# A decoder's first cross attention pipelined two tiles ahead, its bidirectional attention reordered on f16 rows, and filler products in four gaps of TensorE

## The reference, cut to what matters

```python
x = x + gated_linear_attention(ln(x))                    # 4 heads, chunks of 64 tokens here
x = x + cross_attention(ln(x), ctx)                      # 16 heads of 8, softmax over 77 rows
x = x + moe_block(ln(x))                                 # attention over 2 entries, 8 experts
x = x + attention_with_bias(ln(x))                       # 16 heads of 64, softmax over 512
# bidirectional attention; e = ln(x), q = ctx
Sim = (e@w1)[:, :, None] + (q@w2)[:, None, :] + einsum('bid,bjd->bij', e*w3, q) + b_sim
A = softmax(Sim, axis=2);  hq = A @ q
Batt = softmax(max(Sim, axis=2), axis=1);  hc = Batt @ e
x = x + concat([e, hq, e*hq, e*hc]) @ W_qv + b_qv
# feed-forward with fake quantisation
xs = round(e * 32767/amax(e)) / (32767/amax(e))          # 16-bit activations, 8-bit weights
x = x + quantised(gelu(xs @ W_in_q + b_in)) @ W_out_q + b_out
```

## Time and profile before

| | us |
|---|---|
| median of 3 runs | 480.96 |
| the profiled execution, whole | 480.13 |
| its span (what the rows below are in) | 478.3 |
| PE busy in the span | 437.0 (91%) |
| DVE busy | 365.9 (76%) |
| ACT busy | 285.5 (60%) |
| POOL busy | 211.4 (44%) |

### The profile page before, as it was taken

How to read it: one execution, slowest core, us unless ns; L and a number is a source line. 1 busy time by engine, 2 the same in 40 slices (tenths; PEclk the granted TensorE clock), 3 DMA queues, 4 the chain that set the end, 5 groups by cost and what they waited for, 6 DMA issues and landing times.

```text
span 478.3 us, 13019 instructions
## 1 busy us (share of the span) xinstructions
PE 437.0 (91%) x4502; PEld 307.3 (64%) x4502; DVE 365.9 (76%) x987; ACT 285.5 (60%) x669; POOL 211.4 (44%) x545
## 2 busy tenths in 40 slices
PE   7899878887679999699999999999999998999897
PEld 5354446666566777366667676767666665887656
DVE  3867759997868998887778787777778767566766
ACT  3743525565349876577777777777777767413460
POOL 5150011470023458026766767567766767342200
PEclk9979979999979999999999999999999999999999
DMA  7499925500000231000000000000000000000001
GB/s 216 77 98 99 100 32 176 167 14 2 1 0 14 62 93 35 2 1 18 3 19 1 2 16 16 0 0 0 0 0 0 2 1 1 3 3 0 1 1 45
DMA packets 15622, 15.81 MB, mean 33 GB/s; under 512 B 1348, under 2 KB 12859, under 8 KB 15579
## 3 DMA queue, kind: packets, MB, share of 16 engines
q1 hardware_dynamic: 15579, 15.24, 15.7%
HBM read 10.52 MB, written 4.72 MB: 32 GB/s over the span
## 4 chain that ended last, share of the span: by engine, by line
PE 72%; DVE 20%; ACT 4%; issue 3%; DMA 1%; POOL 0%; SPq 0%; DVEq 0%; POOLq 0%
PE bank L951 16%; PE bank L1461 12%; PE bank L1413 10%; PE bank L1336 5%; PE bank L1244 4%; PE bank L1257 3%; PE bank L1454 3%; PE bank L1332 3%; PE bank L1351 2%; DVE PX L1763 2%; DVE mx L1761 2%; PE bank L1573 1%; PE bank L1053 1%; PE bank L1067 1%; DVE Y L1611 1%
## 5 line engine op out<-in xcount | busy, mean ns | idle before, releaser
L855 ACT ACTIVATE SN<-SN,nmx 128x512 f32<-128x512 f32 x128 | 92.7, 724 | 9.8 <-DVE nmx L1975 7.5
L951 PE MATMUL bank<-cs,SN 128*128 128x128 f32 x512 | 67.3, 274 | 3.3 <-DVE Z L1968 1.6
L951 PEld LDWEIGHTS bank<-cs,SN 128*128 128x128 f32 x512 | 57.2, 141 | 18.1 <-issue 12.1
L1413 PE MATMUL bank<-TK,TQ 64*128 64x512 f16 x384 | 52.6, 379 | 1.6 <-DVE TK L1938 1.6
L549 POOL TENSOR_TENSOR CTW<-YT 128x128 f32<-128x128 f32 x64 | 29.6, 462 | 51.6 <-DVE YT L1973 51.1
L1960 DVE CUSTOM_DVE_ANT_0 SN<-bank,strip 128x512 f32<-128x512 f32 x64 | 43.3, 677 | 1.2 <-PE bank L1413 0.6
L1975 DVE CUSTOM_DVE_ANT_0 SN<-bank,strip 128x512 f32<-128x512 f32 x64 | 43.6, 681 | 0.0
L1968 DVE COPY PTO<-bank 128x512 f32<-128x512 f32 x32 | 22.1, 692 | 20.8 <-PE bank L1461 19.2
L866 ACT COPY PTO<-bank 128x512 f32<-128x512 f32 x32 | 18.8, 586 | 26.1 <-PE bank L1461 26.1
L1968 DVE COPY Z<-bank 128x512 f32<-128x512 f32 x32 | 22.1, 691 | 15.9 <-PE bank L1461 14.1
L1461 PE MATMUL bank<-Z,TV 128*64 128x128 f32 x512 | 33.4, 273 | 0.0
(11 more groups left out here) (317 smaller groups left out, 983.9 us busy)
## 6 DMA issues: line engine op xcount, KB each, us to landing
bias_rows<-biasr SPq DMA_DIRECT2D x1, 4096.0 KB, 45.2
band<-bias_rows SPq DMA_DIRECT2D x1, 3072.0 KB, 12.3
wqkv<-in_twqkv SPq DMA_DIRECT2D x8, 192.0 KB, 2.8
w1s<-in_w SPq DMA_DIRECT2D x8, 128.0 KB, 2.3
w2s<-in_w SPq DMA_DIRECT2D x8, 128.0 KB, 3.3
wB<-in_wb SPq DMA_DIRECT2D x1, 753.0 KB, 6.2
wA<-in_wa SPq DMA_DIRECT2D x1, 520.0 KB, 5.1
X<-in_x SPq DMA_DIRECT2D x2, 256.0 KB, 3.2
```

The costliest lines, as they stand in the source:

```text
L855: sc.activation(p, p, ACT.Exp, bias=nmx[:, r % RING, h:h + 1], scale=-1.0, accum_out=psm[:, r % RING, h:h + 1]).then_inc(sm["exp_ready"], 1)
L951: return nc.tensor.transpose(out_, in_, ident[0:n, 0:n])
L1413: ins = mm(bank[2 * (s % 2) + h][:, :], TQ[u][r, q_part, S * b + P * qt:S * b + P * qt + P], TK[u][r, k_part, S * b:S * b + S], start=(k = ...
```

## The change

1. PE: filler products. `keep_busy(5, 3)` ahead of the wait for `bias_ready`, `keep_busy(5, 9)` in place of 4 ahead of `keys_t(0)`, `keep_busy(5, 2)` behind `gla_a(0)`, `keep_busy(3, 8)` ahead of the cross attention's first transposes. In the bidirectional attention `keep_busy(2, 2)` and `keep_busy(7, 2)` go.
2. Cross attention: `xs(1)` goes ahead of the loop and `xs(i+2)` between the second and the third piece of values of tile i. The reciprocal of the sums goes from DVE to ACT as Ln and Exp(-1·). `ctx_norm(i-2)` stands between the maximum and the subtraction of `subtract_max(i)`. `weight_scales` goes, in three parts, to iterations 1 to 3 of the linear attention's loop on DVE.
3. Bidirectional attention: the context's rows and the context times the second block of `W_qv` (plus `b_qv`, whose rows of A sum to 1) are made early, as f16 pairs `CXP` and `CWP`, by two products in the MoE block, a copy on ACT and five operations on POOL at the start of the attention with bias. The attention matrix is an f16 pair (high half ACT, low half DVE). `HQ` and its two copies go, and POOL's addition of `b_qv`. Both matmuls of the context are three f16 products. `weighted_rows` has 128 columns. The orders change.
4. Quantised feed-forward: `WIN` is f16, the quantised rows an f16 pair (`ZP`), each product two f16 matmuls in place of one f32 product. One more DVE operation a group.

```diff
+            keep_busy(5, 3)
             pe.wait_ge(sm["bias_ready"], 1)
...
-            keep_busy(5, 4)
+            keep_busy(5, 9)
             keys_t(0)
...
             gla_a(0)
+            keep_busy(5, 2)
             for i in range(NT):
                 gla_kv(i)
...
+            keep_busy(3, 8)
             norm_half(1, Y, 0)
             queries(0)
             gla_t(1)
             xs(0)
             gla_out(1)
+            xs(1)
             for i in range(NT):
-                if i + 1 < NT:
-                    xs(i + 1)
...
                 for c in range(len(PIECES)):
+                    if c == 2 and i + 2 < NT:
+                        xs(i + 2)
                     pe.wait_ge(sm["pt_ready"], 3 * i + c + 1)
                     times_values(i, c, 0, values)
...  (ACT)
+            def inverse_sums(i):
+                act.wait_ge(sm["xo_mm"], i + 1)
+                if i >= 1:
+                    act.wait_ge(sm["ct_ready"], i)
+                link(sc.activation(rc[:, :], bank[6][:, P:2 * P], ACT.Ln))
+                sc.activation(rc[:, :], rc[:, :], ACT.Exp, scale=-1.0).then_inc(sm["rc_ready"], 1)
             for i in range(NT):
                 act.wait_ge(sm["px_sub"], i + 1)
                 sc.activation(PX[:, i % 2, :, :], PX[:, i % 2, :, :], ACT.Exp, scale=XD ** -0.5).then_inc(sm["px_ready"], 1)
+                if i >= 1:
+                    inverse_sums(i - 1)
                 if i == NT - 1:
                     rstd_of(3, 0)
...
+            inverse_sums(NT - 1)
             rstd_of(2, 0)
...  (DVE)
             def ctx_norm(i):
-                dve.wait_ge(sm["xo_mm"], i + 1)
-                link(vv.reciprocal(rc[:, :], bank[6][:, P:2 * P]))
+                dve.wait_ge(sm["rc_ready"], i + 1)
...
                 link(vv.tensor_reduce(mx[:, :].rearrange("p (j h) -> p j h", h=HG), s4, AX.X, ALU.max))
+                if i >= 2:
+                    ctx_norm(i - 2)
...
-                if i >= 1:
-                    ctx_norm(i - 1)
+                if i == NT - 1:
+                    ctx_norm(NT - 2)
...
-                weight_scales(i - 2)
...  (PE, bidirectional attention)
+                for k, (a_part, c_part) in enumerate(PRODUCTS):
+                    if k == 2:
+                        pe.wait_ge(sm["ast_low"], g + 1)
+                    ins = mm(bank[SIM_BANK[g]][:, :], CXP[:, c_part, g, :], AST[:, g, a_part, :], start=(k == 0), stop=(k == 2))
...
-                    mm(o[:, 2 * P:2 * P + 1], Y[:, t, :], eb[:, t:t + 1], ...)
+                    mm(o[:, 2 * P:3 * P], Y[:, t, :], eb[:, t:t + 1].to_broadcast([P, P]), ...)
...
-                    mm(o, HQ[:, P * i:P * i + P], wB_("qv", P, P), start=first, stop=False, skip_group_check=True)
+                    for k, (a_part, c_part) in enumerate(PRODUCTS):
+                        mm(o, AST[:, g, a_part, c:c + P], CWP[:, c_part, g, :], start=(first and k == 0), ...)
...
-            keep_busy(2, 2)
             tiles_t(TAIL + 3, (NT - 1,), 4)
+            maximum_rows(0)
             attention_t(0)
             pe.wait_ge(sm["ln_yt"], 10 + 3)
             similarity(1, (NT - 1,))
-            maximum_rows(0)
-            keep_busy(7, 2)
-            context_out(0)
             weighted_rows(0)
             maxima_t(1)
-            attention_t(1)
+            context_out(0)
             fused_context(0)
             maximum_rows(1)
-            fused_product(0, range(TG), False)
-            fused_rows(0, True)
+            fused_rows(0, False)
+            attention_t(1)
+            fused_product(0, range(TG), True)
+            weighted_rows(1)
             context_out(1)
-            weighted_rows(1)
...  (DVE, the order after the change)
+            tile_stats((NT - 1,)); maximum_row(0); similarity_sum(0); tile_rows(TAIL + 3, (NT - 1,))
+            similarity_norm(0); maximum_negated(0); similarity_max(1); attention_low(0)
+            similarity_sum(1); maximum_row(1); weighted_norm(0); similarity_norm(1)
+            context_times_norm(0); maximum_negated(1); attention_low(1); bi_residual(0, 0, TG)
+            weighted_norm(1)
             dve.wait_ge(sm["ln_rstd"], TAIL + 4)
             vv.scalar_tensor_tensor(nmr[:, :], ...)
+            context_times_norm(1)
             for k in range(2):
                 bi_residual(k + 1, TG + 2 * k, 2)
...  (PE and DVE, quantised feed-forward)
+                ins = mm(bank[HID_BANK[n % 4]][:, :], WIN[:, P * j:P * j + P], ZP[:, part, S * g:S * g + S], start=(part == 0), stop=(part == 1))
...
-                vv.tensor_scalar(z, z, -32768.0, None, ALU.max).then_inc(sm["zt_ready"], 1)
+                vv.tensor_scalar(hi, z, -32768.0, None, ALU.max).then_inc(sm["zt_ready"], 1)
+                dve.wait_ge(sm["zt_ready"], 2 * g + 1)
+                vv.scalar_tensor_tensor(lo, z, -32768.0, hi, ALU.max, ALU.subtract).then_inc(sm["zt_ready"], 1)
```

More of the change, by code:

```diff
@@ L562, in t5_step @@
                     gp.tensor_tensor(WOP[:, 1, c], WO[:, pair, :], WOP[:, 0, c], ALU.subtract).then_inc(sm["ow_ready"], 1)
+                if s == 1:
+                    pool.wait_ge(sm["cx_copied"], 2)
+                    b = row("b_qv", P, XS).rearrange("p (o d) -> p o d", o=1).to_broadcast([XS, NG, P])
+                    gp.tensor_tensor(CW[:, :, :], CW[:, :, :], b, ALU.add).then_inc(sm["cx_parts"], 1)
+                if 2 <= s < LAG:
+                    part, (dst, src) = s % 2, ((CWP, CW), (CXP, ctxr))[s // 2 - 1]
+                    pool.wait_ge(sm["cx_parts"], 6 + s - 1)
+                    if part == 0:
+                        by = ones[0:XS, 0:P].rearrange("p (o d) -> p o d", o=1).to_broadcast([XS, NG, P])
+                        gp.tensor_tensor(dst[:, 0, :, :], src[:, :, :], by, ALU.mult).then_inc(sm["cx_parts"], 1)
+                    else:
+                        gp.tensor_tensor(dst[:, 1, :, :], src[:, :, :], dst[:, 0, :, :], ALU.subtract).then_inc(sm["cx_parts"], 1)
                 if on(s, 2, last):
@@ L653, in _ @@
             act.wait_ge(sm["vx_ready"], 1)
[L654 removed]
+            sc.activation(KB[:, :], bank[7][:, 0:NG * XS], ACT.Identity, bias=col("bk")).then_inc(sm["cx_copied"], 1)
             act.wait_ge(sm["bias_mm"], 1)
@@ L772, in _ @@
             take_att(1)
-            for g in range(NG):
-                rstd_of(4, g)
+            rstd_of(4, 0)
+            act.wait_ge(sm["cx_mm"], 3)
+            sc.copy(CW[:, :, :], bank[3][0:XS, 0:NG * P].rearrange("p (g d) -> p g d", d=P)).then_inc(sm["cx_copied"], 1)
+            rstd_of(4, 1)
             for g in range(NG):
@@ L1223, in _ @@
             attended_out(1)
+            for g in range(NG):
+                ins = mm(bank[3][0:XS, P * g:P * g + P], wB_("ctxT", XS, XS * g), wB_("qv", P, P), start=True, stop=True)
+            ins.then_inc(sm["cx_mm"], 1)
             keep_busy(5, 7)
@@ L1566, in _, with up @@
             pe.wait_ge(sm["win_ready"], 1)
-            for g in range(NG):
-                pe.wait_ge(sm["zt_ready"], g + 1)
-                for j in range(FB):
-                    n = 4 * g + j
-                    if n >= 4:
-                        pe.wait_ge(sm["ht_ready"], n - 3)
-                    mm(bank[HID_BANK[n % 4]][:, :], WIN[:, P * j:P * j + P], ZT[:, S * g:S * g + S], start=True, stop=True).then_inc(sm["hm_mm"], 1)
+            def up(n, part):
+                g, j = n // FB, n % FB
+                if part == 0 and n >= 4:
+                    pe.wait_ge(sm["ht_ready"], n - 3)
+                pe.wait_ge(sm["zt_ready"], 2 * g + part + 1)
+                ins = mm(bank[HID_BANK[n % 4]][:, :], WIN[:, P * j:P * j + P], ZP[:, part, S * g:S * g + S], start=(part == 0), stop=(part == 1))
+                if part == 1:
+                    ins.then_inc(sm["hm_mm"], 1)
+            for part in range(2):
+                up(0, part)
+                up(1, part)
+            for n in range(2, NG * FB):
+                for part in range(2):
+                    up(n, part)
             keep_busy(1, 7)
@@ L1730, in gla_residual, with weight_scales @@
                 dve.wait_ge(sm["x_done"], g + 1)
+            def weight_scales(part):
+                if part < 2:
+                    dve.wait_ge(sm["ld_c"], 16)
+                    half = slice(FB * part, FB * part + FB)
+                    link(vv.tensor_reduce(amw[:, half], wC[:, F1 * part:F1 * part + F1].rearrange("p (j d) -> p j d", d=P), AX.X, ALU.max,
+                                          apply_absolute_value=True))
+                else:
+                    link(vv.tensor_scalar(amw[:, :], amw[:, :], 1e-8, None, ALU.max))
+                    link(vv.reciprocal(scw[:, :], amw[:, :]))
+                    link(vv.tensor_scalar(scw[:, :], scw[:, :], 127.0, None, ALU.mult))
+                    vv.tensor_scalar(inw[:, :], amw[:, :], 1 / 127.0, None, ALU.mult).then_inc(sm["ws_ready"], 1)
             gla_mask(0)
@@ L2078, in bi_residual @@
                 dve.wait_ge(sm["f_mm"], k + 1)
```

(3 more changed lines are left out.)

111 lines of the change are left out of this document (51 added, 60 removed).

## The result

The changed kernel takes 473.69 us (median of 4, 470.91 to 475.10) against 481.26 us; the ratio is 0.984, with a 95% interval of 0.981 to 0.988. The forecast was 473.3, within 469.8 to 477.2. So the median came out nearly as forecast. The profiled execution took 475.10 us, with a span of 473.3, against 480.13 and 478.3; for an execution like it the forecast was 472.4. Its mean granted clock is 0.978, against 0.979 before. So this pair differs by 5.0 us with the clock equal on average, where the forecast had 3.3 of 7.7 us from the clock (3.3 + 1.3 - 1.3).

What follows compares the result with a forecast made beforehand. Bounds by stage: PE in linear attention and quantised feed-forward, DVE at the bidirectional end, both in turn in the cross attention's loop. 3.3 + 1.3 + 1.3 - 1.3 + 2.1 + 1.0 = 7.7 gained: median 473.3 us (469.8 to 477.2).

Steps and rivals of the forecast that it cites:

- Fillers of the linear attention: Linear attention: new ones products fill PE's idle and remove the clock fall near 26; 3.3 us gained, bounds 0 and 3.4.
- ahead of the cross attention: Ones products fill about 1.8 of 2.65 us of PE's idle and remove the fall there; 1.3 us gained.
- The loop, 2.3 with its start: Cross attention's loop: PE's work decides, weight scales leave DVE, less a stall in iteration 0; 2.3 us gained together.
- 0.26 for each of six tiles: Cross attention's loop: PE's idle for the exponential vanishes, a tile takes 4.27 for 4.53 us; 1.5 us gained.
- The stall in iteration 0: Cross attention's loop: tile 2's scores wait for tile 1's subtraction, ahead of the last piece of values; 0.9 us lost.
- Behind the loop, 1.0 lost: Cross attention's end: ACT runs the last Ln and Exp before the reciprocal deviation; PE's idle 2.65 for 1.69 us.
- The new fall, 1.3: Behind the cross attention's loop: PE's 2.65 us idle brings a new clock fall; 1.3 us lost, between 0.4 and 2.1.
- The third fall, nothing: Clock fall at 131.86, in a stretch the change doesn't fill: costs about 1 us, may stay or go; at nothing.
- Bidirectional attention, 2.1: End of the bidirectional attention: new order gives 2.69, removed fillers 0.86, two low halves cost 0.68 each; 2.1 us gained.
- The rival (nothing): Bidirectional order gives nothing: group 1 starts later, low halves stand on DVE; 2.1 us less gain, 475.4, chance 0.13.
- Quantised feed-forward, 1.0: Quantised feed-forward: PE's product falls to half, ACT is next, GELUs 0.70 to 0.78 us apart; 1.0 us gained.
- The fifth case: Cross attention's loop runs at the low clock because late subtractions idle PE: slower, some 505 us, chance 0.04.

Runs made afterwards that it cites:

- the kernel with the order and nine groups: Changed kernel with the reciprocal deviation ahead of the last inverse sums on ACT and ones products in nine more places: 475.00 us.
- the later groups: Seven groups of ones products behind the cross attention's loop, added to the changed kernel with ACT's two operations there swapped: 471.93 us.
- the kernel with the reordered end: Changed kernel with the reciprocal deviation of the next norm ahead of the last inverse sums on ACT: 470.67 us, ratio 0.979.

## Why the prediction was right, and where not

**Fillers of the linear attention, 3.3, and ahead of the cross attention, 1.3.** Where the falls stood in the kernel before, this came out: A is 2.94 shorter, C 1.38. But the two terms of 4.6 us are worth 2.9 (added alone) and 2.4 (taken away). The step that failed is the one that prices a fall in full from the one execution that showed it. The fall at 26 is absent from 2 of 5 profiled executions without the new products, which with the 2.94 and 1.38 brings 4.6 down to an estimated 3.1. No rival had this. The clock also fell at other places, 54, 198 and 450, which the prediction itself named as a sign of being wrong; that the falls there come in place of the cured ones is not shown (the one at 54 stands in 3 of 5 without the products of the linear attention too).

**The loop, 2.3 with its start.** It gave 3.41. From subtraction to subtraction the six tiles took 5.04, 5.01, 5.51, 4.53, 4.72 and 4.53 us before and 4.08, 4.92, 4.15, 4.52, 4.14 and 4.14 after. So PE's work decides in four of them, as forecast, but at 4.14 us, not 4.27: I subtracted only the one idle that the row of iteration 5 printed. The step mis-sized is "0.26 for each of six tiles". Two tiles gave next to nothing, the one behind the stall (4.92) and the one with PE's idle of 0.45 (4.52), and the first gave 0.96. The tile with the large weight scales gave 1.36 of the 1.7 for both parts; the one with the small ones took 4.53 before, no more than a tile without. The stall in iteration 0, forecast at 0.9, was 0.82. Ln and Exp took 0.62 together, forecast 0.65, and ACT took nothing back from the tiles of 4.14.

**Behind the loop, 1.0 lost.** 1.15 was lost (F), PE's idle 2.51 for 2.65. The named cause, ACT's order, is shown: undoing it gives back 1.46.

**The new fall, 1.3.** It came, at its place, and cost 0.42, at the low end of 0.4 to 2.1. The step mis-sized was that late transposes follow; DVE's chain from the last residual covers nearly all of it. The likeness of idles that it rests on is borne out as a matter of how often: a fall came behind the loop's end in 3 of 3 profiled executions with an idle of 2.51 us there, in 1 of 4 with 1.69, in 0 of 2 with 1.07. So the 1.69 us of the kernel before, read as an idle that is too short for a fall, was one outcome of two.

**The third fall, nothing.** It stayed (129.5). But the earlier trace rows was read as three falls, and there were four; the one at 142, over the experts' first products, was missing in the changed kernel, and H is 0.73 shorter.

**Bidirectional attention, 2.1.** 2.14 in the changed kernel, 2.13 alone. The rival (nothing) falls. The three terms of the sum (2.69 and 0.86 gained, 1.36 lost) are not taken apart by any run, and the end is not quite the one forecast: ahead of the residual of tiles 4 and 5 DVE waits 1.02 us for PE, which itself waited 0.89 us for DVE's `W` (442.05).

**Quantised feed-forward, 1.0.** 1.34 alone, 0.82 with the fall at 450. PE is the bound no more, as forecast. ACT and DVE both work without a pause, each with a spacing of 0.67 where 0.70 to 0.78 were expected, so which of them sets it is not shown. The estimate by the Trainium skill, "ScalarE: Activation LUTs", section on what a table load costs, was 0.706 and a gain of 1.2, the nearer of the two; the measured spacing is below both.

**The sum.** Where no fall disturbs them, loop, bidirectional attention and quantised product give 2.26, 2.14 and 1.34, together 5.7 us; I had 1.3, 2.1 and 1.0, together 4.4. At the same granted clock the two kernels differ by about as much: 475.06 against 480.9 at 0.978 and 0.979, 472.4 against 477.5 at 0.989. The rest of 7.6 us, near 2, is the clock, where I had 4.6 less 1.3. So the total was right by luck: the work was undersized by 1.3 and the clock oversized by as much. The fifth case, a loop at the low clock, did not occur; the nearest to it is the one fall within the loop of the kernel with the order and nine groups, which cost 1.56 us in E.

## What to carry to other kernels

Before pricing a fall of the clock from one profile, look at several executions: cut the timeline into stages, take each stage's time where the clock is up, and judge the clock apart, by its mean over many runs. A fall that one profile shows may be absent from other executions of the same kernel, and curing it is worth that much less. Unread products in many gaps together went with the steadiest clock here (0.996 in four of five), but what the later groups are worth by themselves is not shown. After adding instructions look for idle time with no releaser: with 20 instructions more PE stood still for 2.3 us, and with six of them gone it did not. When an operation is moved to another engine, look at what stands behind it in that engine's order at the end of the loop: here one swapped line was worth 1.5 us.

## What the hardware showed unexpectedly

Executions of one program differ by some 7 us of 480 (477.2 to 484.1 for the kernel before, and 485.4 once), and most of it goes with the mean granted clock (0.972: 482.5 us on average; 0.989: 477.5 us). A fall came with an idle of 1.67 us ahead of 54.85 in the changed kernel, and none with 1.66 us at the same place in the kernel with the reordered end, whose code up to there is the same for PE. At 450.30 one came although PE had been busy for 2.52 of the 3.30 us before. What decides between these is open. How often a fall came goes with the idle of PE ahead of it, over all profiled executions that have the gap:

| PE's idle, us | where | with a fall behind it |
|---|---|---|
| 2.68 | ahead of the cross attention | 5 of 5 |
| 2.51 | behind its loop | 3 of 3 |
| 1.69 | behind its loop | 1 of 4 |
| 1.67 | ahead of the first transposes of the linear attention's output | 4 of 10 |
| 1.45 | ahead of the first transposes of its keys | 3 of 5 |
| 1.07 | behind the loop | 0 of 2 |

These are counts from few executions and from one execution a kernel. And in two kernels PE stood still for 2.29 us at the same instruction with nothing that it waited for, while an instruction packet came at the end of a long transfer (busy share 0.81 to 0.91 of the DMA engines); that it waited for that packet is a reading, not shown.
